# Second layer's row maxima taken over any two neighbouring banks, and put in order of heads later

## What is computed

```python
# second layer, with 16 heads of 8 channels; xn = layernorm(x)
qkv = (xn @ w_qkv).reshape(B, L, 3, H, Dh)
attn = einsum('bhid,bhjd->bhij', q, k) * Dh ** -0.5
attn = softmax(attn + phi_bias(L)[None, None], axis=-1)
out = einsum('bhij,bhjd->bhid', attn, v)          # then w_proj, b_proj
x = x + out + ffn(xn)                             # ffn: W1 (gelu) W2, composed of 32 primitives
```

## Time and profile before

| | |
|---|---|
| runs | 1817.0, 1820.95, 1830.35 us |
| the profiled execution | 1825.96 us, its span 1824.1 us |
| granted TensorE clock, mean | 0.943 of full speed |
| second layer alone | from about 1000 us of the span on; before it the first layer, and three bodies of both together |
| busy | PE 88%, VectorE 79%, ScalarE 71%, GpSimd 51% |

### The profile page before, as it was taken

How to read it: one execution, slowest core, us unless ns; L and a number is a source line. 1 busy time by engine, 2 the same in 40 slices (tenths; PEclk the granted TensorE clock), 3 DMA queues, 4 the chain that set the end, 5 groups by cost and what they waited for, 6 DMA issues and landing times.

```text
span 1824.1 us, 32723 instructions
## 1 busy us (share of the span) xinstructions
PE 1606.0 (88%) x11594; PEld 621.3 (34%) x11594; DVE 1445.2 (79%) x2571; ACT 1287.8 (71%) x2502; POOL 932.1 (51%) x1144
## 2 busy tenths in 40 slices
PE   4798898888888888889879999999999999999995
PEld 2453333333333333333323233232332323323231
DVE  4358778787877878878878888888888888898881
ACT  1227777666766666777667788877888888887885
POOL 2123545554455444555455565555665556564555
PEclk9759989898999989999989999999999999999999
DMA  8313323222223222213232222322222222222200
GB/s 269 58 35 65 71 58 70 55 64 69 71 71 65 70 67 70 71 47 78 63 56 59 55 56 56 59 59 54 56 50 65 59 61 57 54 54 59 60 18 18
DMA packets 133122, 116.36 MB, mean 64 GB/s; under 512 B 16856, under 2 KB 125664, under 8 KB 132960
## 3 DMA queue, kind: packets, MB, share of 16 engines
q1 hardware_dynamic: 126272, 100.64, 23.7%
q0 software_dynamic: 4096, 8.40, 1.4%
q10 hardware_dynamic: 2592, 5.24, 0.9%
HBM read 79.63 MB, written 33.55 MB: 62 GB/s over the span
## 4 chain that ended last, share of the span: by engine, by line
PE 55%; DVE 21%; ACT 10%; issue 4%; DMA 4%; SPq 2%; POOL 2%; another core or an unknown queue 0%; POOLq 0%; ACTq 0%; DVEq 0%
PE pv_acc L630 15%; PE scores_transposed L646 12%; ACT probs L941 5%; PE scores_transposed L774 4%; PE scores_for_max L667 3%; PE scores_transposed L724 3%; DMA stacks<-parts_scratch 3%; DVE maxs L1151 3%; DVE maxs L1178 3%; DVE maxs L1182 2%; DVE xn L1074 2%; PE scores_transposed L746 2%; PE scores_for_max L671 2%; PE scores_for_max L782 2%; PE scores_for_max L683 2%
## 5 line engine op out<-in xcount | busy, mean ns | idle before, releaser
L941 ACT ACTIVATE probs<-scores_transposed 128x512 f32<-128x512 f32 x1664 | 908.9, 600 | 234.7 <-PE scores_transposed L646 221.2
L646 PE MATMUL scores_transposed<-stacks 62*128 62x512 bf16 (+3 forms) x2048 | 575.4, 347 | 61.7 <-ACT probs L941 36.9
L1316 POOL TENSOR_TENSOR probs<-probs,near_bias 128x512 f32<-128x512 f32 x256 | 324.8, 1272 | 360.1 <-ACT probs L941 359.8
L630 PE MATMUL pv_acc<-probs,vals 128*32 128x512 f32 (+3 forms) x4096 | 485.4, 547 | 18.4 <-issue 9.7
L1151 DVE TENSOR_REDUCE maxs<-scores_for_max 128x2 f32<-128x1024 f32 x340 | 409.2, 1221 | 77.9 <-PE scores_for_max L667 75.7
L646 PEld LDWEIGHTS scores_transposed<-stacks 62*128 62x128 bf16 x2048 | 150.5, 94 | 625.6 <-ACT probs L941 298.1
L667 PE MATMUL scores_for_max<-stacks 60*128 60x512 bf16 x1024 | 324.6, 385 | 15.0 <-DVE maxs L1151 8.4
L671 PE MATMUL scores_for_max<-stacks 60*128 60x512 bf16 (+3 forms) x1024 | 262.4, 315 | 37.1 <-DVE maxs L1179 27.0
L1182 DVE TENSOR_REDUCE maxs<-scores_for_max 128x1 f32<-128x512 f32 x256 | 175.0, 684 | 90.8 <-PE scores_for_max L683 79.4
L1154 DVE TENSOR_REDUCE maxs<-scores_for_max 128x1 f32<-128x512 f32 x344 | 226.4, 684 | 25.7 <-PE scores_for_max L667 23.0
L1290 POOL TENSOR_SCALAR_AFFINE_SELECT probs<-probs 128x512 f32<-128x512 f32 x256 | 166.9, 667 | 139.1 <-ACT probs L941 138.6
(11 more groups left out here) (129 smaller groups left out, 2031.4 us busy)
## 6 DMA issues: line engine op xcount, KB each, us to landing
stacks<-parts_scratch SPq DMA_DIRECT2D x768, 64.0 KB
parts_scratch<-parts SPq DMA_DIRECT2D x64, 384.0 KB, 2.6
x_tile<-in_L_attn_x_dram SPq DMA_DIRECT2D x16, 256.0 KB, 2.8
probs<-in_fc_B_dram ACTq DMA_DIRECT2D x1, 4096.0 KB, 19.1
stage_a<-in_fc_A_T_dram SPq DMA_DIRECT2D x1, 4096.0 KB, 16.9
stacks<-mT SPq DMA_DIRECT2D x256, 4.0 KB
x_res<-in_L_attn_x_dram SPq DMA_DIRECT2D x16, 256.0 KB, 3.6
x_tile<-x_between_layers SPq DMA_DIRECT2D x16, 256.0 KB
```

What stands on the lines that cost most here:

```text
L630: last = mm(acc[VW * j:VW * j + VW, q0:T], columns[:, first:first + VW], probs[:, row, column:column + width], start=(kt == 0 and pu % PAI ...
L646: last = mm(st[:, bank, column:column + T - q0], ks[p][rows, h, P * kt:P * kt + P], qs[p][rows, h, q0:T], start=True, stop=True)
L941: fn(probs[:, row, :], st[:, B.use(("st", u, number)).bank, :], ACT.Exp, scale=SCALE).then_inc(s["exp_done"], 1)
L1316: g.tensor_tensor(diag, diag, near_bias[:, kt, :].unsqueeze(1).broadcast_to([P, G, P]), ALU.mult).then_inc(s["emul_pool"], 1)
```

## The change

The order of tiles in the second layer is turned around (query block kt in place of 3 - kt), so that the tile number m itself is the column. Any two tiles that follow one another and lie in neighbouring banks are now reduced together, whether the first is even or odd (`max_groups` goes through the 16 tiles from the left). The columns of `maxs` therefore lie in order of tiles, and GpSimd's two instructions read and write through a four-dimensional view that puts them in the order of heads. The first layer is not touched, nor is the ring of banks.

```diff
@@ beside_tiles
-        e, qt = 1 - j % E, NT - 1 - kt
+        e, qt = 1 - j % E, kt if layer == 1 else NT - 1 - kt
@@ new
+def max_groups(of, su):
+    groups, m = [], 0
+    while m < NT * G:
+        bank = of.use(("max", su, m)).bank
+        n = 2 if m + 1 < NT * G and of.use(("max", su, m + 1)).bank == bank + 1 else 1
+        groups.append((m, n))
+        m += n
+    return groups
@@ VectorE, reduce_tiles(of, su, m)
-                    bank, column = of.use(("max", su, m)).bank, max_column(*BESIDE[1][m])
-                    if m % 2 == 0 and of.use(("max", su, m + 1)).bank == bank + 1:
-                        return
-                    dve.wait_ge(s["s1_ready"], of.packs(1, su, m + 1))
-                    if m % 2 == 1 and of.use(("max", su, m - 1)).bank == bank - 1:
-                        column = max_column(*BESIDE[1][m - 1])
-                        v.reduce_max(maxs[:, su % 2, :].rearrange("p (e x) -> p e x", e=E)[:, :, column],
-                                     s1[:, bank - 1:bank + 1, :], AX_X).then_inc(s["red_done"], 2)
-                    else:
-                        v.reduce_max(maxs[:, su % 2, column:column + 1], s1[:, bank, :], AX_X
-                                     ).then_inc(s["red_done"], 1)
+                    for first, n in max_groups(of, su):
+                        if first + n - 1 == m:
+                            bank = of.use(("max", su, first)).bank
+                            dve.wait_ge(s["s1_ready"], of.packs(1, su, m + 1))
+                            v.reduce_max(maxs[:, su % 2, first:first + n], s1[:, bank:bank + n, :], AX_X
+                                         ).then_inc(s["red_done"], n)
@@ GpSimd, split_max(u)
+                        high, low = msp[:, 0, :], msp[:, 1, :]
+                        if layer == 1:
+                            m = m.rearrange("p (q h e) -> p e h q", q=NT, e=E)
+                            high, low = [x.rearrange("p (e h q) -> p e h q", q=NT, e=E) for x in (high, low)]
-                        g.tensor_copy(msp[:, 0, :], m).then_inc(s["msplit"], 1)
+                        g.tensor_copy(high, m).then_inc(s["msplit"], 1)
-                        g.tensor_tensor(msp[:, 1, :], m, msp[:, 0, :], ALU.subtract).then_inc(s["msplit"], 1)
+                        g.tensor_tensor(low, m, high, ALU.subtract).then_inc(s["msplit"], 1)
```

## The result

The changed kernel takes 1844.58 us (median of 12 runs, 1830.54 to 1850.85), the kernel before, on the same chip, 1822.81 us. The ratio is 1.0117, with a 95% interval of 1.0092 to 1.0143: slower by 1.2%, where I had forecast no change, and above my range of 1806 to 1838 us. The profiled execution took 1844.98 us, 19.0 more than that of before.

What follows compares the result with a forecast made beforehand. TensorE's lines were taken as the main chain, VectorE's pair reduction 5.8% of it. Of 6.8 us saved 0.9 reach the end, pair waits and copies count 0: 1820.95 - 0.9 = 1820.0 us, range 1806 to 1838.

Steps and rivals of the forecast that it cites:

- 106 merges: VectorE's reductions over all 16 batches: 340 pairs and 344 singles become 446 and 132.
- my 6.8 and 15.6 us: VectorE time saved by merging: 6.8 us from start to start, 15.6 us by durations as the upper end.
- GpSimd's copies: GpSimd's small strided instructions: taken as 0 us, at most some 8 us (1828 us) as a rival; chance 0.03.
- unit u = 0 at 15 us: Sign of being right: unit 0 still takes 15.0 us where no half-clock stretch stands.
- the number of reductions is not the pace: Against a rival with VectorE as the pace, 1814 us or 1805 us by durations; chance 0.11.
- the wait of a pair: 94 new pairs with a `pv` burst between their tiles: bounds nothing or 56 us, taken as nothing.
- the claim four tiles on: In the ring of banks, TensorE was said to claim a pair's bank again four tiles later.
- The equal lengths of rows 5: Second layer before the change: second halves 26.18 to 26.19 us, unit 0 14.99 us, whatever the number of reductions.
- the second rival: Units 0 and 1: 41 pairs across a burst lose 0.60 us each, 25 us, giving 1845 us; chance 0.10.
- The granted clock: Half-clock stretches near unit 0, nine at 1.6 us each: none 1805 us, sixteen 1831 us; chance 0.08.

Runs made afterwards that it cites:

- singles_all: Changed kernel with every tile reduced by itself (`n = 1`), no pairs: 1822.99 us, ratio 1.0011 to the kernel before.
- one_pair_a_body: Changed kernel with pairs from even tiles only, as before, plus different odd pairs tried body by body in units u = 2 and 3: one execution 1818.73 us.
- two_pairs_alone: Changed kernel with the old even-tile rule, but in unit u = 2 pair 13-14 where banks allow, and 7-8 in even batches: 1828.53 us, ratio 1.0041 to before.
- pair_7_8_alone: Changed kernel with the old even-tile rule, but pair 7-8 in unit u = 2 of seven even batches: 1819.28 us, ratio 1.0020 to before.
- no_7_8_su0: Changed kernel, new rule, but tiles 7 and 8 of unit u = 2 never a pair: 1835.89 us, ratio 1.0125 to before.
- rest_first: Changed kernel with all 446 pairs, but VectorE makes k's subtraction `rest` ahead of that slot's reduction: 1842.79 us, ratio 1.0104 to before.

## Why the prediction was wrong

What held: 106 merges; a saving on VectorE's reductions between my 6.8 and 15.6 us (their two lines are busy for 409.2 + 226.4 = 635.6 us in the page of before, and 536.7 + 89.7 = 626.4 us after, 9.2 us less, or 0.087 us a merge); GpSimd's copies at no price; unit u = 0 at 15 us; and that the number of reductions is not the pace, which `singles_all` shows from the other side.

The step that failed is in "the wait of a pair": *I take nothing, because the pair needs its time some tiles before its banks are claimed, and VectorE is busy 13.76 to 14.16 us of 14.99 in unit 0, so it is mostly behind.* The bounds were 0 and 56 us, and I took the lower. It measured some 20 us, nearly all of it in unit u = 2 (19.9). Both reasons were read in unit 0 and used for all units. Unit u = 2 differs in three ways. VectorE is busy for only 10.25 us of 12.38 in batch 6, so it was not behind; it could reduce tile 7 as the burst ended, and did. TensorE has little slack there: it is busy for 11.92 us of 12.38. And for the pair 7-8 the distance is shorter: slot 42 puts the q projection into the ring after tile 10, so that the bank of tile 7 is wanted two matmuls sooner than I counted with "the claim four tiles on". I had the projections of q and k in front of me as users of the ring and left them out. The first is what counts most: the pair 3-4 costs 0.67 us over the full distance of four tiles, and in unit u = 3, where TensorE is busy for all of the 13.75 us, it costs nothing because VectorE comes late to it.

The equal lengths of rows 5 misled me in a second way. They showed that the *number* of reductions moves nothing, and that is true. But all pairs there begin with an even tile, so none of them has a burst in its middle, and none stands in front of `rest` of k as 13-14 does. The rows could not price what the change adds. And I had cut halves of a body, not units: within equal halves the units of before differ, 12.82 and 13.37 us in batch 4 against 12.44 and 13.75 in batch 5, so that one unit takes back what the other loses. I wrote that for the second rival ("no row shows one") and still gave it 0.10.

That rival had the right mechanism and the wrong place: I put it into units 0 and 1, since TensorE already waited for L1151 there. That its total (25 us) came out near the loss is luck, since it is 41 other pairs at 0.60 us each. In unit u = 0 the lateness cost nothing: in batch 3's the loads wait 1.2 us for reductions where rows 6 show none, and 3.3 us for exponentials where they show 4.6. The part without a burst, pair 13-14 with 0.82 us a unit (0.44 net of the next), I did not price: I had seen `rest` stand behind a waiting pair, but counted pairs across bursts alone.

The price by kind of batch, from the one-pair runs, against the changed kernel's trace:

| batches | pairs that unit u = 2 gained, us each | sum | measured |
|---|---|---|---|
| 2, 6, 10, 14 | 3-4 0.67; 7-8 0.84; 11-12 0.16; 13-14 0.82 | 2.49 | 2.51 (batch 6) |
| 3, 7, 11 | 11-12 0.16; 13-14 0.82 | 0.98 | 0.99 |
| 4, 8, 12 | 3-4 and 7-8 together 1.67 (batch 8 of one_pair_a_body, 14.49); 13-14 0.22 (`two_pairs_alone` 14.04 less `pair_7_8_alone` 13.82) | 1.89 | 1.89 |
| 5, 9, 13 | 11-12 0.16 | 0.16 | 0.14 |

The granted clock worked as a rival of either sign: three half-clock stretches fewer than before gave back some 5 us of the profiled execution (an estimate, at 1.6 us each).

The rule that "Perfetto Trace Analysis" of the Trainium skill (Optimizing Scalar/DVE Operations) states for smaller instructions fitted this case in part: with single reductions TensorE's instructions of L679 waited 5.3 us for them over the whole run, where those of before waited 33.7, while their waits for VectorE's other work rose from 2.6 to 20.3 us. As a rule for the time it did not decide, since `singles_all` is no faster.

What stays open: what makes an instruction of `xn` four times as long when it meets GpSimd's multiplication, and not at every meeting; and what delays VectorE by 0.5 us at tile 12 in some units. No run took these apart.

## What to carry to other kernels

A merged instruction holds its first buffer until its last input is there, so its price depends on what the producer does between the two inputs and on who takes that buffer next; count the distance in the ring with all its users, not with the main ones alone. Merging saves only its own engine's time, which counts nothing while that engine is not the pace: 106 merges won nothing, and four badly placed pairs in a unit of 12.4 us made it 2.5 us longer. Equal lengths in a trace show that what varied there is free; before using them, check that what the change adds is among what varied.

## What had not been expected

Prices of single waits can add to within 0.02 us over four pairs (12.38 + 0.67 + 0.84 + 0.16 + 0.82 = 14.87, measured 14.89), though in `no_7_8_su0` they miss by 0.5 us, and a body that repeats lets one run make a dozen such trials. The other way about, a wait that is removed need not give anything: `rest_first` made unit u = 2 of batch 6 shorter by 0.83 us and the next one longer by 0.81. And one pair moved can make VectorE meet GpSimd where it did not before: one instruction of `xn` then took 1.29 us in place of 0.34, and the unit 15.27 in place of 14.51.
